# Spreading the q/k and v preparation of the next chunk over all heads of a windowed attention

## What is computed

```python
q, k = l2norm(q) * qs, l2norm(k) * ksc      # 8 heads of 64
q, k = rotary_xpos(q, k)                     # x*c + rotate_half(x)*s, tables by position
# local attention, window 512: block w sees keys of blocks w-1 and w
sim  = einsum('bhwid,bhwjd->bhwij', q * 8, k_lookback)
sim  = where((i < j) | (i > j + 512) | (j == -1), -max, sim)
out  = einsum('bhwij,bhwjd->bhwid', softmax(sim), v_lookback)
x    = x + out @ wo
# then shift_token, layer norm, h @ w1, a * gelu(g), @ w2, residual
```

## Time and profile before

| | us |
|---|---|
| median of 3 runs | 7687.31 |
| the three runs | 7436.9, 7687.31, 7793.86 |
| the profiled execution | 7448.5 |
| its span on the slowest core (5) | 7446.9 |
| spans of the eight cores | 7425.8 to 7446.9 |

### The profile page before, as it was taken

One profiled execution on the slowest core, in us unless ns is written; L12 is line 12 of the kernel. 1 busy time (PEld: TensorE's weight loads), 2 busy tenths in 40 slices (PEclk: granted clock), 3 DMA queues, 4 the chain that ended last, 5 costly groups with the idle time before them and its releaser, 6 DMA issues.

```text
span 7446.9 us, 81984 instructions; the slowest of 8 cores (7425.8 to 7446.9 us)
## 1 busy us (share of the span) xinstructions
PE 4750.5 (64%) x27432; PEld 2738.5 (37%) x27432; DVE 2622.1 (35%) x5073; ACT 1356.0 (18%) x2217; POOL 443.9 (6%) x929
## 2 busy tenths in 40 slices
PE   3545545655666666628888885666666636888888
PEld 1111111111222222207777773222222215667667
DVE  5566564333322222213332332333333212333332
ACT  1222211111222222201111111222222211111111
POOL 1000000120000000010000001000000000000000
PEclk8777777876666666659999997766666658999999
DMA  3000003341000000060101002000000042111110
GB/s 74 23 25 20 19 6 87 136 126 35 26 26 26 26 26 26 12 113 24 35 24 35 24 29 57 26 26 26 26 26 26 12 79 64 52 35 35 52 35 29
DMA packets 169170, 299.57 MB, mean 40 GB/s; under 512 B 29081, under 2 KB 94692, under 8 KB 166712
## 3 DMA queue, kind: packets, MB, share of 16 engines
q0 software_dynamic: 62624, 167.88, 8.7%
q1 hardware_dynamic: 106136, 126.46, 5.5%
HBM read 243.83 MB, written 109.12 MB: 47 GB/s over the span
## 4 chain that ended last, share of the span: by engine, by line
PE 52%; DVE 18%; issue 14%; ACT 8%; DMA 6%; DVEq 1%; POOL 0%; SPq 0%; ACTq 0%; another core or an unknown queue 0%; POOLq 0%
PE psM_ag L98 15%; PE psA_mm L98 8%; PE psM_acc L98 8%; PE psA_on L98 7%; PE psA_sim L98 7%; DVE glx L98 3%; ACT atT L98 3%; PE psB_mm L98 2%; PE psB_stat L98 2%; DVE Sb L98 2%; PE ps_stat L98 2%; ACT sums L98 2%; ACT Sb L98 1%; DVE oT L98 1%; DVE Bx L98 1%
## 5 line engine op out<-in xcount | busy, mean ns | idle before, releaser
L98 PE MATMUL psM_ag<-hbf,w1b 128*128 128x256 bf16 x11264 | 1422.9, 283 | 25.9 <-issue 13.0
L98 PEld LDWEIGHTS psM_ag<-hbf,w1b 128*128 128x128 bf16 x11264 | 1141.4, 102 | 209.5 <-issue 40.4
L98 PE MATMUL psM_acc<-fsc,w2b 128*128 128x256 bf16 x5632 | 774.0, 283 | 381.8 <-DVE fsc L98 381.8
L98 DVE SCALAR_TENSOR_TENSOR fsc<-psM_ag,b1a,glx 128x256 bf16<-128x256 f32 x704 | 336.8, 482 | 1453.8 <-ACT glx L98 1323.1
L98 PEld LDWEIGHTS psM_acc<-fsc,w2b 128*128 128x128 bf16 x5632 | 556.6, 101 | 501.6 <-issue 422.1
L98 ACT ACTIVATE glx<-psM_ag,b1g 128x256 f32<-128x256 f32 x704 | 333.4, 474 | 2072.5 <-PE psM_ag L98 1718.0
L98 ACT ACTIVATE atT<-psA_sim,sb_cpool 128x640 bf16<-128x640 f32 (+4 forms) x512 | 361.2, 756 | 1186.0 <-PE psA_sim L98 1186.0
L98 PE MATMUL psA_on<-atT,vt 128*65 128x512 bf16 x960 | 432.1, 628 | 226.3 <-ACT atT L98 226.3
L98 PE MATMUL psA_mm<-hbf,wqb 128*128 128x512 bf16 x1536 | 401.1, 414 | 193.5 <-DMA xin<-sc_xf 117.4
L98 PE MATMUL ps_mm<-Bx,wk 128*128 128x512 bf16 x512 | 173.1, 499 | 452.1 <-DVE Bx L98 286.8
L98 DVE CAST oT<-psA_on 64x512 bf16<-64x512 f32 x128 | 87.5, 684 | 1051.8 <-PE psA_on L98 1051.8
(11 more groups left out here) (166 smaller groups left out, 5124.2 us busy)
## 6 DMA issues: line engine op xcount, KB each, us to landing
xin<-xT SPq DMA_DIRECT2D x128, 256.0 KB
sc_xm<-SM POOLq DMA_DIRECT2D x128, 256.0 KB, 5.1
xin<-sc_xm SPq DMA_DIRECT2D x240, 128.5 KB
xin<-sc_xf SPq DMA_DIRECT2D x112, 256.5 KB
w1b<-w1l POOLq DMA_DIRECT2D x16, 1365.0 KB, 41.3
sc_x<-SB POOLq DMA_DIRECT2D x64, 256.0 KB, 2.7
sc_xf<-SB POOLq DMA_DIRECT2D x64, 256.0 KB, 2.6
sc_xf<-xz POOLq DMA_DIRECT2D x128, 128.0 KB, 3.0
```

The source lines that it names most:

```text
L98: ins = getattr(h, name)(*a, **k)
```

## The change

`produce_b(c)` becomes `produce_b_thunks(c)`: it emits nothing but returns a list of 16 functions, 8 q/k units (q and k of tile 0, of tile 1, and so on) and then the 8 v units. `consume_heads` takes that list and calls the next two behind each head, after the head's `sums` copy. The loop calls `consume_heads` once over all 8 heads. With 8 heads and 16 units the list is empty at the end, so the loop behind it does nothing. For the last chunk there is no list. `produce_b(0)` at the start stays in one piece.

```diff
-                def produce_b(c):
+                def produce_b_thunks(c):
...
-                    for et in range(4):
-                        for (raw, wbufs, scv, scb, tci, tsi, nbase) in (
-                            (qraw, qw, qs8, "qs8_%d" % l, 0, 1, 0),
-                            (kraw, kw, ks1, "ks1_%d" % l, 2, 3, TC),
-                        ):
+                    thunks = []
+                    def apply_unit(et, raw, wbufs, scv, scb, tci, tsi, nbase, par=None, par3=None):
+                        if True:
...
-                    for hh in range(8):
+                    def vt_unit(hh, par=None, par3=None):
...
+                    import functools
+                    for et in range(4):
+                        thunks.append(functools.partial(apply_unit, et, qraw, qw, qs8, "qs8_%d" % l, 0, 1, 0, par, par3))
+                        thunks.append(functools.partial(apply_unit, et, kraw, kw, ks1, "ks1_%d" % l, 2, 3, TC, par, par3))
+                    for hh in range(8):
+                        thunks.append(functools.partial(vt_unit, hh, par, par3))
+                    return thunks
-                def consume_heads(c, hrng):
+                def consume_heads(c, hrng, thunks=None):
...
+                        if thunks:
+                            for _ in range(2):
+                                if thunks:
+                                    thunks.pop(0)()
...
-                produce_b(0)
+                for th in produce_b_thunks(0):
+                    th()
                 for c in range(NCH):
                     if c + 1 < NCH:
                         produce_a(c + 1)
-                    consume_heads(c, range(0, 4))
-                    if c + 1 < NCH:
-                        produce_b(c + 1)
-                    consume_heads(c, range(4, 8))
+                        tb = produce_b_thunks(c + 1)
+                    else:
+                        tb = []
+                    consume_heads(c, range(0, 8), thunks=tb)
+                    for th in tb:
+                        th()
+                    tb.clear()
                     consume_tail(c)
```

## The result

The changed kernel is slower: 1.0099 times the time of the kernel before, 95% interval 1.0052 to 1.0147. The medians over all runs, 7561.65 us (12 runs) against 7585.17 us (13 runs), don't show it, since they mix in executions in which one die's clock, or both dies', was lower; the ratio leaves these out. The spans of the eight cores in the profiled executions went from 7425.8 to 7446.9 us to 7471.3 to 7499.2 us, 48.6 us more in the mean over the cores.

What follows compares the result with a forecast made beforehand. Attention was taken as a chain of waits that no engine fills, PE busiest at 64%. Per chunk 23.20 + 7.65 - 27.63 + 1.8 = 5.0 us, times 14 = 70 us, on 7448.5 gives 7519 us; range 7436 to about 7800.

Steps and rivals of the forecast that it cites:

- the base: Starting time of the whole kernel's forecast: the profiled execution's own 7448.5 us, to which 70 us were added.
- Removed, 27.63 us: Between heads 3 and 4: without the block of 16 units, QK comes at 2020.44 instead of 2048.07, 27.63 us saved.
- q/k pairs, 4 x 5.80 us: Behind heads 0 to 3: each pair delays the next QK by 5.80 us, 23.20 us a chunk.
- v pairs, 7.65 us: Behind heads 4 to 6: waits for the head's copies plus transposes delay QK by 2.7, 2.25 and 2.7 us.
- The pair behind head 7: The last v pair lies in PE's 9.14 us wait for ACT's logarithm and exp: costs nothing, 2.25 us if not covered.
- The clock, 1.8 us: In the heads: three high-clock stretches a chunk, 0.61 us each, all taken as lost; 0 as the other bound.
- 14 chunks alike: c=0 to 6 in two layers: each changed chunk loses the same 5.0 us, 70 us in all.
- the one of equal times: Whole kernel: changed chunks land 3.6 us better through the clock, so no loss, 7436 to 7468 us; chance 0.19.
- The clock falls in place: Chunk length hangs on where the clock rises; each changed chunk lands 3.6 us better, 7436 to 7468 us; chance 0.19.
- The slower rival: In `produce_a` the clock rises later, more matmul groups stay low at 1.7 us each; over 2% slower, to 7757 us; chance 0.11.
- the faster rival: In attention, heads and units overlap (7062 us), or the clock is high in all heads (7169 us); chance 0.05.

Runs made afterwards that it cites:

- the split version: Kernel before with one q/k unit, cut in two, and one v unit inside each head where PE waits for the exps; 0.9544 of before.

## Why the prediction was right or wrong

Right in mechanism: the loss sits where it was put, behind the heads and in their clock. What failed is the base of the number, said below the terms. The close hit, +0.9% forecast and +0.99% measured (1.0099), is in part luck: the interval reaches from 0.5 to 1.5%, and the spans give 48.6 us, 0.65%, against the 70 forecast. Term by term, per chunk:

- *Removed, 27.63 us*: as read.
- *q/k pairs, 4 x 5.80 us*: measured 5.80, 5.59, 5.59, 5.80, the two shorter ones by a high clock that fell on them. The reading of the chain, with the copies at its head, was confirmed by taking the copies out of it: the distances fell by 0.9 us on the cores shown.
- *v pairs, 7.65 us*: measured 2.28 + 1.81 + 2.29 = 6.38. This term was mis-sized. The wait for the copies was right (5.32 us behind av's start by the forecast, 2058.49 - 2053.17 = 5.32 in the trace), but the transposes hold PE for only 0.49 us (2058.49 to 2058.98), not 0.70 to 1.10: the first figure is a modelled duration, and the second had VectorE's pace in it. The start of the next instruction is the price, as the prediction itself had used it elsewhere. Behind head 5 the same: 1.81 us, below the range of 2.1 to 2.35. The v part loses 1.21 us, not 2.48: the largest miss in the sum.
- *The pair behind head 7*: hidden, as forecast; the wait for ACT shrank to 6.76 us.
- *The clock, 1.8 us*: about right, 2.0 us measured inside the heads, over all cores and middle chunks. The way to it was not: three high stretches a chunk were counted and all taken as lost; over all middle chunks there were 3.7 a chunk before, and 1.3 are left. High clock still falls on the changed kernel, partly on pairs where it helps little (the 0.38 us matmuls above).
- *14 chunks alike*: the two c=0 chunks lost 2.04 us, not 3.4, and that no rows had been read for them is part of the 70 against 49.

The step that failed is the base. The 7519 us was the profiled execution's 7448.5 plus 70, while the median shown was 7687.31 us; against that, the same number reads as 2% faster, the opposite of what the sum says and of the 1% slower that was measured. The step "a median of the changed kernel can lie in the same spread as the runs shown" widened the range but left the number on a base of its own; the sum should have been given as a difference and put on the median's base as well. The median itself was no firm base: with 13 runs in place of 3 it was 7585.17 us.

Of the rivals, the one of equal times did not happen. "The clock falls in place" had one thing right, chunk lengths still vary, but not its sum: from one chunk's statistics to the next it takes 191.4 to 196.3 us on core 5 of the changed kernel, where it took 187.7 to 192.7 on core 5 before, so the whole range moved up. The slower rival, `produce_a` at a low clock, cost nothing that the changed kernel's trace shows: statistics to next head 0, all cores, moved by 0.1 us a chunk. The two halves of the faster rival were real levers that this change does not pull: overlap was possible (0.9544), but only with the units where PE waits, and so was the high clock in the heads (0.9772 even in the changed order), but only with matmuls that fill the waits. The advice of the Trainium skill, page "TensorE: Matmul & The Clock Gate", section "Why this matters for your kernels", to avoid long idle gaps between bursts, is borne out by these runs in its direction. Already two waits of 1.72 us a head went with a granted clock of about 0.6 (0.59 over heads 0 to 3 in the earlier trace rows), and waits of about 1 us with 1.00. The prediction had read it as speaking for the change; cutting one thin stretch into seven makes more gaps, not fewer, and the clock inside the heads went from 0.64 to 0.52.

## What to carry to other kernels

To hide a side chain beside a main one on an in-order engine, put its instructions where the main chain already waits for another engine, and split it so that its own waits fall there too (the split was worth nothing in heads of 10.5 us and 1.8 us a head in those of 6.4); between two pieces of the main chain that would have followed each other without a gap, every wait of it is paid, each time. When a block is cut up, count what each cut puts in front (here the head's two copies, 1 us) before counting what it hides. And price short instructions by the distance to the next start, not by their modelled duration.

## What the runs showed of the hardware that had not been expected

Matmuls whose results nobody reads made the changed kernel 2.3% quicker than the kernel before, and took the split version from 0.9544 to 0.9134 of before: with the waits in the heads filled down to about 1 us or less, the granted clock went from 0.60 to 1.00 and the 8 av matmuls from 3.60 to 1.89 us. Without them, in the kernel before, bursts of 4.8 us of the same av and QK matmuls with waits of 1.72 us between the groups left the clock at its low level for most of the time (0.64 in the mean from a head's first QK to its av).
